# Tanh attention: scores on 64-row halves, products in three parts placed later, transposes and projection later

## The reference

```python
q = _make_heads(query, H)
k = _make_heads(key, H)
v = _make_heads(value, H)
u = jnp.einsum('hbqd,hbkd->hbqk', q, k) * scale / np.sqrt(d_k)
logits = jnp.tanh(u) * jnp.exp(log_C)
logits = jnp.where(mask, -jnp.inf, logits)
attn = jax.nn.softmax(logits, axis=-1)
out_heads = jnp.einsum('hbqk,hbkd->hbqd', attn, v)
out = jnp.moveaxis(out_heads, 0, -2).reshape(query.shape)
return out @ W_out.T
```

## Time and profile before

| what | value |
|---|---|
| median of 3 runs | 3672.95 us (3671.74 to 3675.34) |
| profiled execution, its own time | 3672.53 us |
| its span | 3670.8 us |
| PE matmul busy | 2872.7 us, 78% of the span |
| DVE, ACT, POOL busy | 1500.6, 1074.4, 292.5 us |
| mean granted TensorE clock | 0.875 of 2.4 GHz |

### The profile page before, as it was taken

How to read it: one execution, slowest core, us unless ns; L and a number is a source line. 1 busy time by engine, 2 the same in 40 slices (tenths; PEclk the granted TensorE clock), 3 DMA queues, 4 the chain that set the end, 5 groups by cost and what they waited for, 6 DMA issues and landing times. The chain is left out here.

```text
span 3670.8 us, 48289 instructions
## 1 busy us (share of the span) xinstructions
PE 2872.7 (78%) x15310; PEld 2137.1 (58%) x15310; DVE 1500.6 (41%) x5309; ACT 1074.4 (29%) x2159; POOL 292.5 (8%) x338
## 2 busy tenths in 40 slices
PE   4774189996699979699999999927997199999232
PEld 3663167775466745456666666626886077777121
DVE  5886312222211123423333333430111666666777
ACT  3442011110355421033334333302221044444121
POOL 0000300002311100000000000021001211110000
PEclk8896589998799879899999999958998599999555
DMA  2111132211111100100000000025553100000000
GB/s 73 42 48 60 36 139 92 76 61 35 54 34 33 34 30 0 55 9 9 5 8 8 8 8 4 1 88 183 179 180 118 54 26 18 18 18 7 23 0 20
DMA packets 62362, 174.11 MB, mean 47 GB/s; under 512 B 13387, under 2 KB 32601, under 8 KB 52793
## 3 DMA queue, kind: packets, MB, share of 16 engines
q1 hardware_dynamic: 52184, 148.10, 12.2%
q0 software_dynamic: 10080, 24.79, 2.2%
HBM read 143.50 MB, written 29.36 MB: 47 GB/s over the span
## 5 line engine op out<-in xcount | busy, mean ns | idle before, releaser
L2077 PE MATMUL L_ffne_up<-L_ffne_xT,L_ffne_wu 128*128 128x280 f32 (+1 forms) x1696 | 406.1, 398 | 23.1 <-DVE L_ffne_xT L2003 15.6
L2077 PEld LDWEIGHTS L_ffne_up<-L_ffne_xT,L_ffne_wu 128*128 128x128 f32 x1696 | 324.9, 193 | 94.7 <-ACT L_ffne_hT L1990 16.7
L1212 PEld LDWEIGHTS L_xattn_o<-L_xattn_v,L_xattn_pt 125*112 125x112 f32 x3072 | 335.8, 178 | 42.2 <-issue 14.8
L1212 PE MATMUL L_xattn_o<-L_xattn_v,L_xattn_pt 125*112 125x64 f32 (+1 forms) x3072 | 328.2, 251 | 0.0
L1063 DVE TENSOR_REDUCE L_xattn_least<-L_xattn_s 112x1 f32<-112x375 f32 x256 | 128.4, 543 | 473.0 <-PE L_xattn_s L1192 472.8
L2063 PE MATMUL L_ffne_dn<-L_ffne_wd,L_ffne_hT 128*128 128x256 f32 (+1 forms) x1312 | 288.0, 379 | 1.6 <-issue 1.6
L1199 PEld LDWEIGHTS L_xattn_pt<-ident,L_xattn_p 112*125 112x125 f32 x1536 | 186.7, 188 | 138.0 <-issue 138.0
L2063 PEld LDWEIGHTS L_ffne_dn<-L_ffne_wd,L_ffne_hT 128*128 128x128 f32 (+1 forms) x1312 | 240.8, 184 | 44.7 <-issue 2.4
L1147 PE MATMUL L_xattn_job<-L_xattn_ctxT,L_xattn_wk 128*128 128x375 f32 x640 | 233.0, 493 | 2.2 <-DMA L_xattn_msk<-in_mask 1.0
L1076 DVE COPY L_xattn_pt<-L_xattn_pt 125x336 f32<-125x336 f32 x512 | 234.2, 499 | 1.0 <-PE L_xattn_pt L1199 1.0
L1199 PE MATMUL L_xattn_pt<-ident,L_xattn_p 112*125 112x112 f32 x1536 | 232.2, 287 | 0.0
(11 more groups left out here) (318 smaller groups left out, 3875.4 us busy)
## 6 DMA issues: line engine op xcount, KB each, us to landing
L_ffne_wd<-in_L_ffn_down SPq DMA_DIRECT2D x29, 1024.0 KB, 4.9
L_ffne_wu<-in_L_ffn_up SPq DMA_DIRECT2D x21, 1024.0 KB, 5.4
L_ffne_wu<-in_L_ffn_up SPq DMA_DIRECT2D x8, 2048.0 KB, 8.0
L_xattn_ctxT<-in_ctxT SPq DMA_DIRECT2D x32, 375.0 KB, 3.1
fa_ctxT<-in_ctxT SPq DMA_DIRECT2D x16, 375.0 KB, 6.1
fa_rows<-in_ctx_rows SPq DMA_DIRECT2D x16, 375.0 KB
ta_kT<-in_ctxT SPq DMA_DIRECT2D x16, 375.0 KB
ta_ctxr<-in_ctx_rows SPq DMA_DIRECT2D x16, 375.0 KB
```

The lines of the kernel that those rows point to most:

```text
L1212: m = pe.matmul(o, pt_sb[:, head % 4, kt, :], v_sb[:, h, kt, hd, :], start=(kt == 0), stop=(kt == KT - 1))
L2077: m = pe.matmul(up_ps[s % RING][k][:, 0, 0:RH], wu[:, h, c, k * FF + f * 128:k * FF + (f + 1) * 128], xT[:, h, c, q * RH:(q + 1) * RH], st ...
```

## The change

A chunk's two matmuls take 64 partitions each: the query is multiplied with `halfmask` (four heads on each half of the partitions), `qbd` is half as large, and the key tile is cut into its upper and lower 64 rows. Each of the two contracts over 64 rows and writes the same bank as before, 448 columns.

Products come in three parts of 3, 3 and 2 heads (18, 18 and 12 records). In PE's order they, the transpose of the output and the projection stand later: batch b now has scores 0, products of b - 1 group 0 part 1, projection of b - 2, scores 1, part 2, transpose of x for b + 1, scores 2, group 1 part 0, scores 3, part 1, scores 4, part 2, scores 5, products of b group 0 part 0, transpose of the output of b - 1. On DVE `finish` is split into `take_onT` and `residual`; the residual of b - 2 comes first in batch b, then the copy of the transposed query, then `head_mean` and `take_onT` of b - 1.

```diff
@@ -527,7 +527,7 @@
         hide_b = sb("hide_b", [KP, 2, KT])
         xn = sb("xn", [S, 2, D])
         xt = sb("xt", [128, 2, DC, S])
-        qbd = sb("qbd", [128, 2, DC, HG, S])
+        qbd = sb("qbd", [128, 2, DC, HG // 2, S])
         kT = sb("kT", [128, 2, DC, SK])
         ctxr = sb("ctxr", [KP, 2, KT, D])
         vaug = sb("vaug", [KP, 2, KT, H, DH + 1])
@@ -578,8 +578,8 @@
                     after(pool, s_out, (b - 1) * CH)
                     for c in range(DC):
                         q = pool.tensor_tensor(
-                            qbd[:, h, c, :, :], xt[:, h, c, :].unsqueeze(1).broadcast_to([128, HG, S]),
-                            core.headmask[:, :].unsqueeze(2).broadcast_to([128, HG, S]), ALU.mult)
+                            qbd[:, h, c, :, :], xt[:, h, c, :].unsqueeze(1).broadcast_to([128, HG // 2, S]),
+                            core.halfmask[:, :].unsqueeze(2).broadcast_to([128, HG // 2, S]), ALU.mult)
                     q.then_inc(q_done, 1)
                     pool.wait_ge(ctx_in[h], 16 * (b - h) + 32)
                     after(pool, pv_out, 2 * (b - 1))
@@ -643,11 +643,13 @@
                     dve.tensor_tensor(on[:, h, :].rearrange("p (h d) -> p h d", h=H), o[:, :, 0:DH],
                                       rec[:, :].unsqueeze(2).broadcast_to([S, H, DH]), ALU.mult).then_inc(on_done, 1)
 
-                def finish(b, h, ch):
+                def take_onT(b, h):
                     dve.wait_ge(onT_out, b + 1)
                     after(dve, y_out, b - 1)
                     dve.tensor_copy(onT[:, h, :, :], fin_ps[:, 0, 0:DC * S].rearrange(
                         "p (c s) -> p c s", c=DC)).then_inc(onT_done, 1)
+
+                def residual(b, h, ch):
                     dve.wait_ge(y_out, b + 1)
                     dve.tensor_tensor(core.xs[:, h, :], fin_ps[0:S, 0, 0:D], x[:, b, :],
                                       ALU.add).then_inc(y_done, 1)
@@ -655,22 +657,25 @@
                     core.keep(ch, dve, b, h)
 
                 def body(b, h):
+                    low = b if isinstance(b, int) else NB
                     if not isinstance(b, int) or b < NB - 1:
                         normalize(b + 1, 1 - h)
-                    first = isinstance(b, int) and b == 0
-                    ch = Chain(dve, chain, (b - 1) * PER)
-                    if not first:
-                        head_mean(b - 1, 1 - h, ch)
+                    ch = Chain(dve, chain, 0 if low < 2 else 1 + (b - 2) * PER)
+                    if low >= 2:
+                        residual(b - 2, h, ch)
                     if not isinstance(b, int) or b < NB - 1:
                         take_xt(b + 1, 1 - h)
-                    if not first:
-                        finish(b - 1, 1 - h, ch)
+                    if low >= 1:
+                        head_mean(b - 1, 1 - h, ch)
+                        take_onT(b - 1, 1 - h)
                 normalize(0, 0)
                 take_xt(0, 0)
                 each_batch(dve, body)
-                ch = Chain(dve, chain, (NB - 1) * PER)
+                ch = Chain(dve, chain, 1 + (NB - 2) * PER)
+                residual(NB - 2, 0, ch)
                 head_mean(NB - 1, 1, ch)
-                finish(NB - 1, 1, ch)
+                take_onT(NB - 1, 1)
+                residual(NB - 1, 1, ch)
 
             @block.tensor
             def _(pe):
@@ -686,8 +691,9 @@
                     g, kt = c // KT, c % KT
                     after(pe, tanh_done, b * CH + c - 1)
                     for j in range(2):
-                        m = pe.matmul(s_ps[c % 2][0:KP, j, 0:GT], kT[:, h, g, kt * KP:(kt + 1) * KP],
-                                      qbd[:, h, g, 4 * j:4 * j + 4, :], start=True, stop=True)
+                        r = slice(64 * j, 64 * j + 64)
+                        m = pe.matmul(s_ps[c % 2][0:KP, j, 0:GT], kT[r, h, g, kt * KP:(kt + 1) * KP],
+                                      qbd[r, h, g, :, :], start=True, stop=True)
                     m.then_inc(s_out, 1)
 
                 def products(b, h, g, part):
@@ -697,13 +703,13 @@
                         pe.wait_ge(v_done, b + 1)
                         if g == 0:
                             after(pe, on_done, b - 1)
-                    for hh in range(part * HG // 2, (part + 1) * HG // 2):
+                    for hh in range(part * 3, min(part * 3 + 3, HG)):
                         head = g * HG + hh
                         for kt in range(KT):
                             m = pe.matmul(o_ps[h][0:S, 0, head * (DH + 1):(head + 1) * (DH + 1)],
                                           pT[:, h, g, kt, hh * S:(hh + 1) * S], vaug[:, h, kt, head, :],
                                           start=(kt == 0), stop=(kt == KT - 1))
-                    if part == 1:
+                    if part == 2:
                         m.then_inc(pv_out, 1)
 
                 def transpose_o(b, h):
@@ -722,33 +728,41 @@
                     m.then_inc(y_out, 1)
 
                 def body(b, h):
-                    first = isinstance(b, int) and b == 0
+                    low = b if isinstance(b, int) else NB
                     last = isinstance(b, int) and b == NB - 1
                     pe.wait_ge(ctx_in[h], 16 * (b - h) + 32)
                     pe.wait_ge(q_done, b + 1)
                     scores(b, h, 0)
+                    if low >= 1:
+                        products(b - 1, 1 - h, 0, 1)
+                    if low >= 2:
+                        project(b - 2, h)
                     scores(b, h, 1)
-                    if not first:
-                        products(b - 1, 1 - h, 1, 0)
-                    scores(b, h, 2)
-                    if not first:
-                        products(b - 1, 1 - h, 1, 1)
+                    if low >= 1:
+                        products(b - 1, 1 - h, 0, 2)
                     if not last:
                         transpose_x(b + 1, 1 - h)
+                    scores(b, h, 2)
+                    if low >= 1:
+                        products(b - 1, 1 - h, 1, 0)
                     scores(b, h, 3)
-                    if not first:
+                    if low >= 1:
+                        products(b - 1, 1 - h, 1, 1)
+                    scores(b, h, 4)
+                    if low >= 1:
+                        products(b - 1, 1 - h, 1, 2)
+                    scores(b, h, 5)
+                    products(b, h, 0, 0)
+                    if low >= 1:
                         transpose_o(b - 1, 1 - h)
-                    scores(b, h, 4)
-                    products(b, h, 0, 0)
-                    if not first:
-                        project(b - 1, 1 - h)
-                    scores(b, h, 5)
-                    products(b, h, 0, 1)
                 transpose_x(0, 0)
                 pe.wait_ge(w_in, 64)
                 each_batch(pe, body)
-                products(NB - 1, 1, 1, 0)
-                products(NB - 1, 1, 1, 1)
+                products(NB - 1, 1, 0, 1)
+                project(NB - 2, 0)
+                products(NB - 1, 1, 0, 2)
+                for part in range(3):
+                    products(NB - 1, 1, 1, part)
                 transpose_o(NB - 1, 1)
                 project(NB - 1, 1)
```

## The result

The change makes the kernel slower: 3773.0 us (median of 4) against 3674.1 (4 runs of the kernel before), a ratio of 1.0267, 95% interval 1.0249 to 1.0284. The profiled executions stand at 3771.3 and 3672.5 us, 98.8 us apart.

The account below looks back on a forecast made before the run. TensorE's own work sequence was taken to bound the stage. Sixteen batches of 31.9 us at low clock, 512 us with tail waits, less 20, give 492, 111 more than 380.8: 3672.5 + 111 = 3784 us, range 3555 to 3806.

Parts of the forecast that it names:

- case A: Tanh attention: TensorE's clock is low nearly throughout, 31.9 us a batch, 111 us more, 3784 us; chance 0.57.
- What bounds: Tanh attention stage, 380.8 us: TensorE's own sequence of work sets its end, 21.43 us per batch at full clock.
- The pair: A chunk's scores on row halves, two matmuls at a time: 0.98 us at full clock instead of 1.50.
- the bound of 1.69: Lower bound in us for a chunk's paired scores at 1.2 GHz, giving 30.3 us a batch.
- The clock: TensorE between chunks: with wide scores halved and narrow products left, the clock falls and hardly rises; granted clock near 0.5.
- B: Rival for the stage: a pair counts as two streams and the clock holds; 271 us, 110 us less, 3563 us; chance 0.28.
- What I took off for stretches at full clock: Stage sum: 20 us subtracted from 512 for dense places where the clock rises, 1.3 batches' worth at 15.5 us.
- my 492: Forecast stage time in us: sixteen slow batches with the tail's waits, 512, less 20 for dense places.
- The waits: Both gaps ahead of products (1.20 us a batch) go; the POOL, DVE and SP queues cost nothing.
- The rule that names idle gaps: Trainium skill rule on TensorE's clock: with no idle gaps left it would stay up, 110 us less, 3563 us.
- D: Rival for the scores: a pair's two matmuls don't run together; 19.6 us a batch, stage 351 us, 3643 us; chance 0.03.
- C: Rival for the stage: the clock goes back and forth, 8 to 12 batches low, 3679 to 3741 us; chance 0.12.

Follow-up runs that it names:

- e3: The changed kernel with each pair of score matmuls issued twice, the second over the first; 3649.1 us, ratio 0.9933 to the kernel before.
- e5: The changed kernel with both score matmuls of a chunk on the same 64 rows; 3948.2 us, ratio 1.0746 to the kernel before.
- e1_order_only: The changed kernel's new order, but with scores over full 128 rows as before; 3610.4 us, ratio 0.9828 to the kernel before.
- e6_chunk_1_halved: e1_order_only with chunk 1 alone on row halves, its half-size query built on POOL; 3614.5 us, ratio 0.9840 to the kernel before.

## Why the prediction was right

The forecast was 3784 us, slower, by case A; measured 3773.0.

- What bounds: right. TensorE's own sequence set the stage, before (gaps of 1.2 us a batch) and after (none).
- The pair: 0.95 us at 2.4 GHz where I had 0.98 with the weights ahead of it; part of what I counted there is at the block behind it, 1.87 us for 18 records instead of 1.7. At 1.2 GHz the pair costs 1.79 us, under the 1.96 that I took and over the bound of 1.69. The products cost 0.191 instead of 0.182 us a record, and the transposes 1.09 instead of 0.8 us a batch. The errors cancel, which is luck: a batch of 32.09 us against 31.9.
- The clock: right, and now with more of its reason. A pair doesn't count as two streams. I had that open, with 0.28 for B. The result rules B out, e3 shows that it is the wide work that is missing, and e5 that rows count. Case B's 2.4 GHz doesn't come, though B's condition that no idle gap be left is met.
- What I took off for stretches at full clock was too small. Sixteen batches of 32.09 us and 1.3 us of waits in the tail would be 515 us; the stage takes 474.7, so by this sum the eight stretches at 2.4 GHz, 3.4 to 10.2 us long, are worth 40 us and not 20. That term of the sum was half of what it should be. The first comes from the opening, where chunks stand with no products between them; the others begin where projection and chunk 1 have stood together, which is the place I had named. The timeline of PE at the third, which begins at 1058.5:

```profile
1055.34 2.03 PE L726 MATMUL ta_fin_ps<-ta_wo,ta_onT 128*112 128x256 f32 x4
1057.30 1.58 PE L695 MATMUL ta_s_ps<-ta_qbd,ta_kT 64*125 64x448 f32 x4
1058.81 1.35 PE L709 MATMUL ta_o_ps<-ta_vaug,ta_pT 125*112 125x17 f32 x12
...
1063.15 1.02 PE L695 MATMUL ta_s_ps<-ta_qbd,ta_kT 64*125 64x448 f32 x4
1064.11 2.49 PE L709 MATMUL ta_o_ps<-ta_vaug,ta_pT 125*112 125x17 f32 x18
```

  After two chunks of 0.95 us the clock falls again within the products of 1064.11. These 20 us, less what the batch and the tail were off, are the 17 us by which the stage came out lower than my 492, and with the 5 us outside the stage, which I didn't have, the 12 us by which 98.8 differs from 111.
- The waits: right for steady batches. PE waits for ACT only in batch 0, 1.2 us in all, because scores stand there without products. POOL's value copy waits for the last products of the batch before (151.9 us in 14 waits), and nobody waits for it, as worked out.
- The rule that names idle gaps (the Trainium skill, TensorE: Matmul & The Clock Gate, section Why this matters for your kernels) would have kept the clock up here. The trace after disagrees: 472.2 of 474.7 us busy, and 0.55.
- The other rule, up to 2x from row tiling (the Trainium skill, TensorEngine Tiling (Array Packing), section Theoretical Speedup), holds as an upper end: 1.50 / 0.95 is 1.6x for the chunk at the same clock.
- D: its pairs do overlap (1.02 us for four records in the row of 965.39).
- Slips in the working that decide nothing: behind the last chunk stand 96 product records (72 before), and the 78 (48) are those behind the last batch's queue. The ends of A's range, by the terms given for them, are 3758 and 3804 us. In C the times leave out the 7 us of the tail that B's 271 us have.

What I didn't see is that the two halves of the change go opposite ways. The order by itself is worth 66 us (3676.6 to 3610.4 on one chip), and the row halves cost 77 us on the old order and 163 us on the new one (3773.0 against 3610.4, on two chips; by the ratios to the kernel before, 161 us).

## What to carry to other kernels

Before a packing that halves TensorE's streaming time, look at what stands between. Here 17-column matmuls took 9.2 of the 19.7 us of a batch in e1_order_only, about as long as the loads of their weights (160.5 and 167.4 us in the stage). The wide ones held the clock at 2.4 GHz, and packing them all nearly doubled everything else. Pack one place at a time, first where wide work lies on both sides, and read the granted clock of the stage rather than its busy time, which said 99% here in the slow kernel. Closing TensorE's idle gaps can be worth more than the gaps, if the wide work stays: e1_order_only took 1.73 us off a batch at full clock, 28 us in all, and the stage became 58 us shorter.

## What the runs showed of the hardware

- Rows count for TensorE's clock. 24 records of 448 columns over 64 rows, 18.6 us of them, leave it at 1.2 GHz; 12 such records over 128 rows raise it within 7.4 us, and in the changed kernel pairs on both halves do within 5.7 us. I had this as one of two open theories.
- More matmul work can be faster: each score pair issued twice, 3649.1 against 3773.0 us.
- It tips. From no halved chunk to one costs next to nothing (ratios 0.9828 and 0.9840 to the kernel before), the second behind it costs 78 us (3614.5 to 3692.6), and all six cost 163 us. Two at other places, with other products beside them, cost nothing and gain (3600.5 against 3615.0 us).
- A pair on row halves costs about 0.1 us at its neighbours: the projection ahead of chunk 1 takes 1.03 instead of 0.94 us to the next start, and 12 records behind it 1.20 instead of 1.11. So a halved chunk that looks worth 0.56 us (0.94 instead of 1.50) is worth 0.37, as the batches of 19.33 and 19.70 us say. The rows are e6_chunk_1_halved, then e1_order_only:

```profile
1103.00 1.10 PE L731 MATMUL ta_fin_ps<-ta_wo,ta_onT 128*112 128x256 f32 x4
1104.03 1.02 PE L700 MATMUL ta_s_ps<-ta_qhf,ta_kT 64*125 64x448 f32 x4
1104.97 1.35 PE L714 MATMUL ta_o_ps<-ta_vaug,ta_pT 125*112 125x17 f32 x12
1106.17 0.39 PE L690 MATMUL ta_xt_ps<-ident,ta_xn 112*128 112x112 f32 x2
```

```profile
1102.03 1.10 PE L725 MATMUL ta_fin_ps<-ta_wo,ta_onT 128*112 128x256 f32 x4
1102.97 1.67 PE L694 MATMUL ta_s_ps<-ta_qbd,ta_kT 128*125 128x448 f32 x4
1104.47 1.26 PE L708 MATMUL ta_o_ps<-ta_vaug,ta_pT 125*112 125x17 f32 x12
1105.58 0.39 PE L686 MATMUL ta_xt_ps<-ident,ta_xn 112*128 112x112 f32 x2
```
